# GpSimd's product with C and its sum into y as two instructions over two blocks each, in a state-space scan that VectorE, TensorE and GpSimd share

## The chip, the cores and the metric

The kernel runs on 1 core of one Trainium2 chip. The metric is the device time of one launch in microseconds (us). Engines are named as in the profile: PE is TensorE, ACT is ScalarE, DVE is VectorE, POOL is GpSimd, SP is SyncE, which only issues DMAs here. SBUF is the on-chip memory of 128 partitions, PSUM the accumulator memory of eight banks.

## The reference

Two layers on 4096 tokens (2 sequences of 2048) of width 256. The first layer is a selective scan and a mixture of four experts, the second is an attention with 16 heads and a feed-forward net. The part that the change touches is the scan:

```
A_bar = exp(delta[..., None] * A)                  # decay, 512 channels x 16 states
Bx = delta[..., None] * Bm[:, :, None, :] * xb[..., None]
def step(h, inp):
    a_t, bx_t, c_t = inp
    h = a_t * h + bx_t
    y_t = jnp.sum(h * c_t[:, None, :], axis=-1)    # the sum over the 16 states
    return (h, y_t)
...
y = y + xb * Dp
out = y * jax.nn.silu(z) @ W_out                   # gate, then project
```

The sum over the states of h times C is what GpSimd computes.

## The kernel before

The first phase works on eight chunks of 512 tokens. The 512 channels of a chunk are four blocks of 128 partitions, so h, y, the decays and the like are tiles of 128 x 4 x 512 in float32, the four blocks side by side in each partition. Each engine runs its own program, written out by hand: for iteration i it goes through the 16 states n = 0 to 15 of chunk i, and between the states it does its share of the side work for the chunk after (f = i + 1: convolution, projections, delta), the chunk before (m = i - 1: gate, output projection, router and experts) and the one before that (q = i - 2: queries, keys, values). All waits are on semaphores; nothing is scheduled at run time.

For each chunk c and state n:

- ACT writes the decays of four blocks (L948), two states ahead at most.
- PE broadcasts row n of B to 128 partitions in PSUM (L603).
- DVE multiplies it with delta times x for each block (`b_times`, L1264) and scans each block over its 512 tokens (`scan`, L1273) into `h[:, n % 2]`. There are two buffers of h. The first scan of state n waits until GpSimd has added state n - 2 to y. After the fourth block `keep_state` (L1278) keeps the last column.
- SP loads row n of C as a broadcast into `c_sb[:, n % 2]`, once the product of state n - 2 is made.
- GpSimd waits for all four scans, multiplies h with C in place (`times_c`, L1486), and adds the products to y (`add_y`, L1497). The last instruction of each tells of the whole, so nothing waits for one block.

Between the states DVE has side work that reads and writes SBUF: `gated` (L1288, y times the gate, 2048 elements), `crossed` (L1367), the keys' scaling in `keys` (L1376, two instructions), `weigh` (the router's weights: L1319, six comparisons at L1325, L1333, on 4 to 16 elements), `split_bias` (L1383 to L1389, four instructions of 512 elements on 16 partitions), `split_bc` (L1239 to L1246, five of 512) and `deltas` (L1254 and L1256, twice each, 1024 elements). The order around them is

```
if n == 7 and inside(m):
    weigh(m)
...
if n == 9 and inside(q):
    split_bias(q)
```

GpSimd has side work too: the splitting of q and k into bfloat16 parts (L1550 to L1559, 1024 elements) and short steps of the norms (L1566 to L1571).

When the eight chunks are done, a short stretch finishes the last experts, and from about 1850 us the attention and the feed-forward net run, in which GpSimd only copies values (L227) and adds a bias (L2019 and L2023, 1024 elements).

Of the kernel before, what the change touches and what calls it, by code (L numbers as in the profile page):

```python
# [11 lines left out]
ALU = mybir.AluOpType  # L12
# [3 lines left out]
P = 128  # L16
B, L, D = 2, 2048, 256
TOK = B * L
CH = 512
# [5 lines left out]
DB = DI // P  # L25
# [209 lines left out]
C_RING = 2  # L235
# [6 lines left out]
def mamba_moe_qkv(nc, a, scr, sh, chunks=NCH):  # L242


    with ExitStack() as ctx:  # L245
        def sb(name, shape, dt=F32):
            return ctx.enter_context(nc.sbuf_tensor(name, shape, dt))
# [42 lines left out]
        y = sh.heads_v[:].rearrange("p (b t) -> p b t", b=DB)  # L290
        decay = blocks_of[:, 0:2 * CH * DB].rearrange("p (a b t) -> p a b t", a=2, b=DB)
        h = sh.vals[:, 0:2 * CH * DB].rearrange("p (a b t) -> p a b t", a=2, b=DB)
        c_sb = sb("c_sb", [P, C_RING, CH])
# [1185 lines left out]
        def _(pool):  # L1479
            def times_c(c, n):  # L1480
                pool.wait_ge(c_loaded[n % C_RING], 16 * (c * (NS // C_RING) + n // C_RING + 1))
                pool.wait_ge(s["h_ready"], (c * NS + n + 1) * DB)
                if (c + 1) % CB:
                    pool.wait_ge(s["state_kept"], (c - c // CB) * NS + n + 1)
                for m in range(DB):
                    last = nc.gpsimd.tensor_tensor(h[:, n % 2, m, :], h[:, n % 2, m, :],  # L1486
                                                   c_sb[:, n % C_RING, :], ALU.mult)
                last.then_inc(s["hc_ready"], 1)

            def add_y(c, n):  # L1490
                pool.wait_ge(s["hc_ready"], c * NS + n + 1)
                if n == 0:
                    pool.wait_ge(s["y_begun"], (c + 1) * DB)
                else:
                    pool.wait_ge(s["y_added"], c * NS + n)
                for m in range(DB):
                    last = nc.gpsimd.tensor_tensor(y[:, m, :], y[:, m, :], h[:, n % 2, m, :], ALU.add)  # L1497
                last.then_inc(s["y_added"], 1)

            def first_values():  # L1500
# [72 lines left out]
            def iteration(i):  # L1573
                f, m, q = i + 1, i - 1, i - 2
                for n in range(NS):
                    if inside(i):
                        times_c(i, n)
                    if n == 0 and inside(q):
                        scale("ln2", q)
                    if n == 1 and inside(m):  # L1580
                        scale("ln1", m)
                    if n == 12 and inside(i + 2):
                        scale("ln0", i + 2)
                    if inside(i):
                        add_y(i, n)
                    if n == 1 and inside(f):
                        mix_edge(f)
                    if n == 6 and inside(f):
                        add_edge(f)
                    if n == 8 and isinstance(i, int) and i == chunks:  # L1590
                        first_values()
                    if 4 <= n < 8 and inside(q):
                        split(q, 0, q_f[:], n - 4)
                    if 9 <= n < 13 and inside(q):
                        split(q, 1, k_f[:], n - 9)
# [525 lines left out]
```

## Time and profile before

| | before |
|---|---|
| median of 3 runs | 3641.55 us (3640.53 to 3644.67) |
| the profiled execution, its own time | 3645.86 us |
| its span in the profile | 3644.1 us |
| PE busy in the span | 3312.8 us (91%) |
| DVE busy | 2839.1 us (78%) |
| ACT busy | 2176.2 us (60%) |
| POOL busy | 1527.7 us (42%), nearly all of it before 1640 us |
| mean granted clock of PE | 0.963 of full |
| POOL L1486, product with C | 512 instructions, 681.5 us |
| POOL L1497, sum into y | 512 instructions, 648.0 us |

The shares are averages over phases that have different limits. The phase that the change touches lasts from about 68 to 1620 us, and is read by itself below. An instruction's duration in the profile includes time in which it had begun and stood.

### The profile page before, as it was taken

Reading aid. Unit: us, or ns where it says so; the run is one execution under the profiler, and the core shown is the slowest. Engines: PE = TensorE matmul, PEld = TensorE weight load, DVE = VectorE, ACT = ScalarE, POOL = GpSimd, SP = SyncE. Lnnn points to the kernel's source line nnn. Section 1 sums busy time; section 2 is a strip of 40 time slices with the busy share of each in tenths; the row PEclk is TensorE's granted clock in tenths of the full one; section 3 lists DMA queues with packets and bytes.
Section 4 is the critical chain, followed back from the end, with each engine's and each line's share of the span. In section 5 each row is a group of like instructions: output and inputs, shape, how many; then the busy total and the mean of one; then the engine's idle time right before and its main releaser. Section 6 shows DMA issues by size and latency. Waiting matters only on the chain. (4 is left out here: it accounts for less than half of the span.)

```text
span 3644.1 us, 41261 instructions
## 1 busy us (share of the span) xinstructions
PE 3312.8 (91%) x14448; PEld 1552.3 (43%) x14448; DVE 2839.1 (78%) x3484; ACT 2176.2 (60%) x3604; POOL 1527.7 (42%) x1294
## 2 busy tenths in 40 slices
PE   4239999999999999989889999999999999998998
PEld 2025556555655555555522222322222222222666
DVE  5898899999989899974468888888888888882444
ACT  5355666656565756532157777777777777777221
POOL 2998899999999999971010000000000000000110
PEclk8679999999999999999999999999999999999999
DMA  3111223131222212232020000000000000000010
GB/s 109 32 38 52 73 70 102 63 112 64 94 84 82 87 62 93 73 121 85 26 97 19 19 19 19 19 17 17 15 17 19 19 19 19 19 10 7 23 35 29
DMA packets 108187, 180.19 MB, mean 49 GB/s; under 512 B 13989, under 2 KB 81689, under 8 KB 99417
## 3 DMA queue, kind: packets, MB, share of 16 engines
q1 hardware_dynamic: 107992, 177.72, 15.5%
q8 instruction: 108, 1.77, 0.2%
q14 instruction: 87, 0.70, 0.1%
HBM read 151.58 MB, written 26.08 MB: 49 GB/s over the span
## 5 line engine op out<-in xcount | busy, mean ns | idle before, releaser
L1927 DVE TENSOR_REDUCE tile_max<-ps 128x1 f32<-128x1024 f32 x976 | 1149.9, 1220 | 248.2 <-PE ps L1723 248.2
L1866 ACT ACTIVATE probs<-ps 128x512 f32<-128x512 f32 x2048 | 1106.4, 598 | 375.4 <-PE ps L1736 373.8
L1486 POOL TENSOR_TENSOR vals<-vals,c_sb 128x512 f32<-128x512 f32 x512 | 681.5, 1363 | 131.9 <-DVE state L1278 111.0
L1273 DVE TENSOR_TENSOR_SCAN vals<-stacks,state,ps 128x512 f32<-128x512 f32 x512 | 655.0, 1279 | 103.0 <-POOL heads_v L1497 38.1
L1736 PE MATMUL ps<-stacks 101*128 101x512 bf16 x2048 | 701.8, 382 | 24.7 <-PEq L245 12.2
L1497 POOL TENSOR_TENSOR heads_v<-heads_v,vals 128x512 f32<-128x512 f32 x512 | 648.0, 1298 | 8.7 <-issue 0.2
L1723 PE MATMUL ps<-stacks 99*128 99x512 bf16 x1952 | 583.8, 380 | 0.0
L227 POOL COPY heads_v<-vals 128x256 f32<-128x256 f32 x32 | 12.7, 402 | 1344.7 <-PE ps L1746 1322.2
L1746 PE MATMUL ps<-probs,heads_v 128*32 128x512 f32 x4096 | 545.3, 605 | 0.0
L731 PE MATMUL ps<-x1T,e_w 128*128 128x512 f32 x1024 | 464.1, 599 | 26.2 <-ACT hid L1041 26.2
L1736 PEld LDWEIGHTS ps<-stacks 101*128 101x128 bf16 x2048 | 195.7, 96 | 658.9 <-ACT probs L1866 423.2
L755 PE MATMUL ps<-e_w,hid 128*128 128x256 f32 x2048 | 455.0, 380 | 10.8 <-DVE x_tok L1355 8.8
L755 PEld LDWEIGHTS ps<-e_w,hid 128*128 128x128 f32 x2048 | 390.0, 191 | 84.7 <-issue 31.5
L1041 ACT ACTIVATE hid<-ps,cols 128x512 f32<-128x512 f32 x288 | 192.2, 687 | 390.1 <-PE ps L731 376.4
L731 PEld LDWEIGHTS ps<-x1T,e_w 128*128 128x128 f32 x1024 | 192.0, 191 | 261.0 <-issue 210.3
L1723 PEld LDWEIGHTS ps<-stacks 99*128 99x128 bf16 x1952 | 191.4, 98 | 172.5 <-issue 1.9
L948 ACT ACTIVATE stacks<-stacks,neg_a 128x512 f32<-128x512 f32 x256 | 167.0, 713 | 60.7 <-DVE vals L1273 60.2
L948 ACT ACTIVATE stacks<-vals,neg_a 128x512 f32<-128x512 f32 x256 | 166.3, 712 | 55.8 <-DVE vals L1273 50.3
L1264 DVE TENSOR_TENSOR ps<-soft,ps 128x512 f32<-128x512 f32 x256 | 177.2, 692 | 11.4 <-PE ps L603 3.2
L1264 DVE TENSOR_TENSOR ps<-stacks,ps 128x512 f32<-128x512 f32 x256 | 177.3, 693 | 7.0 <-issue 0.2
L2023 POOL TENSOR_TENSOR y<-x,b 128x1024 f32<-128x1024 f32 x8 | 19.3, 2417 | 377.6 <-DVE x L88 377.6
L603 PE MATMUL ps<-bc,sel 96*128 96x512 bf16 x128 | 52.1, 409 | 126.5 <-DVE ps L1264 112.1
(201 smaller groups left out, 3055.1 us busy)
## 6 DMA issues: line engine op xcount, KB each, us to landing
e_w<-in_e_w SPq DMA_DIRECT2D x64, 1024.0 KB, 7.1
c_sb<-scratch_c SPq DMA_DIRECT2D x128, 256.0 KB, 3.4
stacks<-scratch_q SPq DMA_DIRECT2D x192, 64.0 KB
stacks<-scratch_k SPq DMA_DIRECT2D x192, 64.0 KB
scratch_q<-parts SPq DMA_DIRECT2D x16, 384.0 KB, 4.2
scratch_k<-parts SPq DMA_DIRECT2D x16, 384.0 KB, 4.4
xr<-scratch_x SPq DMA_DIRECT2D x10, 512.0 KB, 4.4
xn_tok<-in_x SPq DMA_DIRECT2D x8, 512.0 KB, 4.9
```

The source lines that it names most:

```text
L731: last = mm(bank(key), e_w1[:, e % 2, k, i * P:(i + 1) * P], x1T[:, k, :], start=k == 0, stop=k == KD - 1)
L755: last = mm(ps[:, DOWN_BANK[at], i * D:(i + 1) * D], hid[:, k, (2 * pair + i) * P:(2 * pair + i + 1) * P], e_w2[:, e % 2, k, :], start=k = ...
L948: fn(decay[:, n % 2, m, :], deltas_at[c % 2][:, m, :], ACT.Exp, scale=neg_a[:, n * DB + m:n * DB + m + 1]).then_inc(s["decay_ready"], 1)
L1264: v.tensor_tensor(ps[:, 0, :], dus_at[c % 2][:, m, :], ps[:, 2 + n % 2, :], ALU.mult).then_inc(s["bx_ready"], 1)
L1273: v.tensor_tensor_scan(h[:, n % 2, m, :], decay[:, n % 2, m, :], ps[:, 0, :], state[:, n, m:m + 1], ALU.mult, ALU.add).then_inc(s["h_ready ...
L1486: last = nc.gpsimd.tensor_tensor(h[:, n % 2, m, :], h[:, n % 2, m, :], c_sb[:, n % C_RING, :], ALU.mult)
L1497: last = nc.gpsimd.tensor_tensor(y[:, m, :], y[:, m, :], h[:, n % 2, m, :], ALU.add)
L1723: last = mm(ps[:, at + i, :], qs[0:K_MAX, u % ROT, t * P:(t + 1) * P], ks[0:K_MAX, u % ROT, k * CH:(k + 1) * CH], start=True, stop=True)
L1736: mm(ps[:, S_BANK[i], :], ks[0:K_ALL, j, step * P:(step + 1) * P], qs[0:K_ALL, j, qc * CH:(qc + 1) * CH], start=True, stop=True).then_inc( ...
L1746: last = mm(ps[qc * VW:(qc + 1) * VW, AV_BANK, :], vh[:, u % ROT, step, :], probs[:, step % 2, qc, :], start=step == 0, stop=step == KT - 1)
L1866: fn(probs[:, step % 2, qc, :], ps[:, S_BANK[i], :], ACT.Exp)\
L1927: v.tensor_reduce(tile_max[:, t, half:half + 1], ps[:, at:at + PAIR, :].rearrange("p a n -> p (a n)"), AX.X, ALU.max).then_inc(s["max_read ...
```

## The change

The four instructions of 512 elements per partition in `times_c` become two of 1024, and so do the four in `add_y`. C is read with a repeat over the two blocks. Elements, order of the states, waits and semaphore counts stay as they are.

```diff
-                for m in range(DB):
-                    last = nc.gpsimd.tensor_tensor(h[:, n % 2, m, :], h[:, n % 2, m, :],
-                                                   c_sb[:, n % C_RING, :], ALU.mult)
+                for m in range(0, DB, 2):
+                    last = nc.gpsimd.tensor_tensor(h[:, n % 2, m:m + 2, :], h[:, n % 2, m:m + 2, :],
+                                                   c_sb[:, n % C_RING:n % C_RING + 1, :].to_broadcast([P, 2, CH]),
+                                                   ALU.mult)
                 last.then_inc(s["hc_ready"], 1)
...
-                for m in range(DB):
-                    last = nc.gpsimd.tensor_tensor(y[:, m, :], y[:, m, :], h[:, n % 2, m, :], ALU.add)
+                for m in range(0, DB, 2):
+                    last = nc.gpsimd.tensor_tensor(y[:, m:m + 2, :], y[:, m:m + 2, :], h[:, n % 2, m:m + 2, :],
+                                                   ALU.add)
                 last.then_inc(s["y_added"], 1)
```

## Rows read from the trace of the kernel before

**Rows 1.** The page: busy time of the engines, and the loads of C.

```profile
PE 3312.8 (91%) x14448; PEld 1552.3 (43%) x14448; DVE 2839.1 (78%) x3484; ACT 2176.2 (60%) x3604; POOL 1527.7 (42%) x1294
...
c_sb<-scratch_c SPq DMA_DIRECT2D x128, 256.0 KB, 3.4
```

**Rows 2.** Busy time in two stretches; the columns are PE, PEld, DVE, ACT, POOL.

```profile
430.00:1430.00 1000.00, 955.48 (x3200) 570.70 (x3199) 914.01 (x1143) 624.05 (x911) 931.99 (x776) 0.99 0.26 82
1430.00:1620.00 190.00, 173.89 (x595) 109.06 (x595) 158.47 (x186) 93.48 (x135) 179.04 (x146) 0.95 0.26 82
```

**Rows 3.** What DVE waited for, 430 to 1430 us: total, times, longest.

```profile
DVE vals L1273 <- POOL heads_v L1497: 12.2, 10, 2.2
DVE vals L1273 <- ACT stacks L948: 10.8, 6, 2.2
DVE x_tok L1355 <- PE ps L755: 7.8, 5, 2.4
DVE vals L1254 <- ACT soft L1012: 2.3, 2, 1.3
```

**Rows 4.** What PE waited for longest, 430 to 1430 us.

```profile
PE ps L731 <- ACT hid L1041: 21.1, 15, 1.7
```

**Rows 5.** POOL's instructions in order of time, states 1 and 2 of chunk 4.

```profile
851.87 4.96 POOL L1486 TENSOR_TENSOR vals<-vals,c_sb 128x512 f32<-128x512 f32 x4 [1.41 <-DVE state L1278]
...
869.66 4.97 POOL L1497 TENSOR_TENSOR heads_v<-heads_v,vals 128x512 f32<-128x512 f32 x4
```

**Rows 6.** DVE's in order of time: the first scan of state 4.

```profile
874.66 1.28 DVE L1273 TENSOR_TENSOR_SCAN vals<-stacks,state,ps 128x512 f32<-128x512 f32 x1 [2.09 <-POOL heads_v L1497]
```

**Rows 7.** POOL lines one by one: least, median and greatest duration in ns.

```profile
L1571 POOL TENSOR_TENSOR ln_t<-ln_half,ln_r x24: 200/203/204, 8.2 to 1805.8; 128x4 f32<-128x4 f32 x24
```
```profile
L1497 POOL TENSOR_TENSOR heads_v<-heads_v,vals x512: 1255/1270/2261, 73.6 to 1615.8; 128x512 f32<-128x512 f32 x171
```
```profile
L2023 POOL TENSOR_TENSOR y<-x,b x8: 2348/2353/2865, 3350.3 to 3596.1; 128x1024 f32<-128x1024 f32 x8
```
```profile
L1553 POOL TENSOR_TENSOR q_f<-q_f,parts x8: 2122/2136/2304, 506.9 to 1829.7; 128x1024 f32<-128x1024 f32 x8
```

**Rows 8.** DVE's L1385, its durations, and once beside a POOL instruction of 1024 elements.

```profile
L1385 DVE TENSOR_TENSOR soft<-soft x5: 680/1647/2489, 548.1 to 1841.2; 16x512 f32<-16x512 f32 x5
```
```profile
1841.20 2.49 DVE L1385 TENSOR_TENSOR soft<-soft 16x512 f32<-16x512 f32 x1
```
```profile
1840.94 2.21 POOL L1553 TENSOR_TENSOR k_f<-k_f,parts 128x1024 f32<-128x1024 f32 x1
```

**Rows 9.** DVE in order of time: the weights of the router, chunk 4.

```profile
921.37 0.91 DVE L1319 TENSOR_TENSOR prob<-lexp,lmax 128x16 f32<-128x16 f32 x1
922.32 3.76 DVE L1325 TENSOR_TENSOR beats<-prob 128x12 f32<-128x12 f32 x6
...
926.41 0.95 DVE L1333 SCALAR_TENSOR_TENSOR cw<-rank,prob 128x16 f32<-128x16 f32 x1
```

**Rows 10.** POOL in order of time, the same stretch and after.

```profile
920.99 4.99 POOL L1486 TENSOR_TENSOR vals<-vals,c_sb 128x512 f32<-128x512 f32 x4 [0.18 <-DVE state L1278]
926.05 4.96 POOL L1497 TENSOR_TENSOR heads_v<-heads_v,vals 128x512 f32<-128x512 f32 x4
...
946.66 6.24 POOL L1486 TENSOR_TENSOR vals<-vals,c_sb 128x512 f32<-128x512 f32 x4
```

**Rows 11.** Other side work of DVE line by line: least, median, greatest in ns.

```profile
L1288 DVE TENSOR_TENSOR gate<-heads_v,gate x8: 2293/2880/2889, 242.5 to 1617.1; 128x2048 f32<-128x2048 f32 x8
```
```profile
L1376 DVE TENSOR_SCALAR k_f<-k_f,temp x16: 475/958/2344, 511.3 to 1839.2; 128x512 f32<-128x512 f32 x16
```
```profile
L1241 DVE TENSOR_TENSOR q_f<-bc_f,bc x8: 689/1643/1645, 36.0 to 1376.9; 96x512 f32<-96x512 f32 x8
```
```profile
L1256 DVE TENSOR_TENSOR stacks<-stacks,vals x8: 1224/2172/2181, 52.5 to 1211.5; 128x1024 f32<-128x1024 f32 x8
```

**Rows 12.** What DVE waited for, 242 to 430, 68 to 242 and 1430 to 1620 us.

```profile
DVE x_tok L1355 <- PE ps L755: 4.3, 2, 3.4
DVE vals L1273 <- ACT stacks L948: 3.0, 2, 1.8
```
```profile
DVE vals L1273 <- POOL heads_v L1497: 12.4, 8, 2.8
```
```profile
DVE vals L1273 <- POOL heads_v L1497: 11.8, 7, 3.6
```

## The prediction, made before the changed kernel ran

> **What bounds the kernel now.** I read the page first: PE is busy for 91% of the span and POOL for 42% [rows 1], but POOL's work with C lies in the first phase, so I went on to busy times by stretch. Between 430 and 1430 us, five periods of 200 us in the middle of the scan, PE is busy for 955 us of 1000, POOL for 932 and DVE for 914 [rows 2]. Three engines near their limit: the waits must say which of them ends last. DVE's list shows 12.2 us on POOL's sum, 10.8 and 2.3 us on ACT and 7.8 us on PE [rows 3], with small rests some 37 us, 7.4 us a period: 2.4 on POOL and 4.9 on ACT and PE. Its other idle time, 86 - 37 = 49 us, is the gap of about 0.1 us between its instructions. PE's longest wait is for ACT's gelu [rows 4], which itself waits its turn behind decays.
>
> In order of time the period reads so. In states 1 to 3 POOL is behind: its products and sums run without a gap from 851.87 to 874.63, and the first scan of state 4 waits 2.09 us for the sum of state 2 [rows 5, 6]. In states 5 to 15 the path runs over PE and ACT, and DVE follows with 4.9 us of slack. So POOL sets the end in a short part of each period, and DVE is 5 us away from setting the rest.
>
> **What the change saves on POOL.** Instructions on float32 take 203 ns for 4 elements, 1270 for 512, 2353 for 1024 [rows 7]. The first two give (1270 - 203) / 508 = 2.10 ns an element, and 203 + 2.10 x 1020 = 2345 for 1024, which is the third. So the cost is per element, with a fixed part. Four in a row take 4.96 us [rows 5]: one starts every (4.96 - 1.27) / 3 = 1.23 us. Two make 2.46; one of 1024 takes a turn of 2.35 less the overlap of 0.04, 2.31. The saving is 0.15 us for each pair. The other bound is the 1024 elements of L1553, 2.13 us, whose second input is bfloat16 [rows 7]: 2.09 a turn, 0.37 us a pair. I take 0.15, since L2023 has float32 on all sides, as here.
>
> There are 512 pairs, 79 us of POOL's time, but only those in stretches where POOL is behind count. In a period these are the 16 instructions from 851.87 to 874.63 (two products, two sums of four) [rows 5]: 8 pairs, 1.2 us. In the first and the last chunk, where DVE waits for POOL 12.4 and 11.8 us [rows 12], I count half of the 128 instructions, 32 pairs or 4.9 us each; in chunk 1 some 11 pairs, 1.7 us. Together 4.9 + 1.7 + 5 x 1.2 + 4.9 = 17.5 us. With 0.37 a pair it would be 42 us.
>
> The loads of C cost nothing new: each is issued when a product ends, lands in 3.4 us [rows 1], and is wanted two products and two sums of waiting later, over 9 us with the longer instructions too. Nothing waits for single blocks, before or after.
>
> **What it costs on DVE.** DVE's side work takes longer beside POOL than alone. L1385 takes 680 ns alone, 1647 as a rule in the loop, and 2489 where a POOL instruction of 1024 elements had begun just before it [rows 8]. That POOL instruction ended at 1840.94 + 2.21 = 1843.15, and L1385 at 1843.69: it stood for 1.95 us and ran for 0.54. So it stands until POOL's instruction is over, whatever its length, and then runs. POOL's next one stands in turn: four products took 6.24 us in place of 4.96 at 946.66, where the four of `split_bias` ran [rows 10]. They alternate. Each DVE instruction behind such a turn loses what POOL's turn lasts, and this doubles: +1.08 us (2.35 less 1.27). One that comes at any moment loses half a turn on average, +0.54.
>
> By this, one period's side work:
> - `weigh`: product and sums run from 920.99 to 931.01, while L1319, the six at L1325 and L1333 take 5.99 us from 921.37 to 927.36 [rows 9, 10], on tiles of at most 16 elements. The six go in twos at each end of a POOL instruction. With instructions of 1024 the ends come at 923.3, 925.7, 928.1 and 930.5, so they finish near 931.1: +3.8.
> - `split_bias`, four in a row: the first stands behind a sum's end that comes 0.6 us sooner, three lose 1.08: +2.6.
> - `split_bc`, five, L1241 among them at 1643 for 689 alone [rows 11]: one stands behind a cast that stays short; three lose 1.08, and the first, which now slips in front of a POOL instruction, loses a little: +3.4.
> - `deltas`: L1256 stands at 2172 for 1224 alone [rows 11]; twice 1.08 and, for the two L1254, twice 0.54: +3.2.
> - `keys`, L1376, 2 x 1.08, as its one 2344 ns beside L1553 shows: +2.2. `gated`, at 2880 for 2293 [rows 11], begins just behind a product: +1.1. `crossed`: +0.5.
>
> The sum is 16.8 us. POOL will be at work for less of the time, so I take 0.9 of it, 15. The lower bound goes with the 2.13 us instruction, 0.86 in place of 1.08: 12.
>
> A rule bears on this, and speaks against the change. The Trainium skill (SBUF — State Buffer, section "Who interferes with whom") says that a VectorE instruction with two SBUF inputs contends with a GpSimd one that reads SBUF, and that whoever comes first keeps the pair of ports for its whole instruction. The trace agrees with 2489 against 1647 ns. By a rule in which the two only shared bandwidth, the length of an instruction would not matter, and the sum would be the saving alone, 17.5 us faster.
>
> **The sum.** A period of the five in the middle: +15 on DVE, less the 4.9 us that it waits for ACT and PE today, less 1.2 from POOL: +8.9. As a check: DVE's busy 183 + 15, its small gaps 9.8 and what is left of the wait on POOL, 1.2, make 209 against 200. Five of them: +45. Chunk 1 has no `keys` and no `split_bias`: (1.1 + 3.8 + 3.4 + 3.2) x 0.9 = 10.4, against 4.3 + 3.0 us [rows 12] and 6.3 of smaller waits on PE and ACT: covered, about 0 with POOL's 1.7. The first chunk has `split_bc` and `deltas` for the next: 5.9 - 4.9 = +1. The last has `keys`, `weigh`, `split_bias`: 7.7 - 4.9 = +2.8. Together +49 us. The attention is untouched. The profiled execution took 3645.86, 4.3 over the median of 3641.55; 3645.86 + 49 = 3695, and against the median 3690.5. I say 3690.
>
> **The rivals.** A change within 0.2% (7 us) can't be told from none.
> - *The saving decides, faster.* The place is the same side work: if DVE's slack swallows the longer stands, the time falls by 17.5 us, to 3624; with 0.37 a pair, to 3600. It decides once the added stands stay under 4.9 + 1.2 = 6.1 us a period, below 0.4 of what I count. For it: 4.9 us of slack, and POOL idle more often. Against it: a dozen of the instructions stand in chains, where POOL always has the next one ready. 0.12.
> - *The short 1024.* With 2.09 us a turn the period gives 12 - 4.9 - 2.9 = +4.2, five of them 21, and the ends -7, -4 and -6: +4, 3646. For it L1553, against it the line through three float32 rows. 0.08.
> - *Nothing is absorbed.* The stands fall where PE and ACT then wait for DVE's scans in turn: 16.8 - 1.2 = 15.6 a period, 78, and 10, 1 and 3 for the ends: 3734. PE's 45 us idle in 1000 [rows 2] would become over 100. 0.15.
> - My forecast, with a partial absorption of either sign: 0.65.
>
> **How the numbers follow.** The likeliest case has its own range from 3660, where half of the stands beyond the slack vanish, to 3725. The range of 8 in 10 goes from 3628 to 3735: it takes in the short 1024 and the upper case, and leaves out most of the faster one. Faster 0.12, same 0.08, slower 0.65 + 0.15 = 0.80.
>
> **What would show each step.** The product and the sum should have 256 instructions each, near 2350 ns; near 2130 would be the second rival. L1385 and L1241 should stand at 2.7 us, L1256 at 3.2, the six of L1325 near 7 us together for 3.76. POOL's busy time between 430 and 1430 should fall by 4 to 8 us in 100, DVE's should rise, and DVE's waits on PE and ACT nearly vanish, with PE idle longer. If L1385 stays at 1.65 us beside instructions of 1024, the whole cost side is wrong and the first rival holds. If the stands are as said and the period stays at 200 us, the slack was larger than DVE's waits show.

## The result, and the profile after

| | before | after |
|---|---|---|
| median | 3642.2 us (4 runs, 3640.53 to 3644.67) | 3699.39 us (4 runs, 3697.43 to 3702.77) |
| ratio after/before | | 1.0157, 95% interval 1.0141 to 1.0173 |
| span of the profiled execution | 3644.1 us | 3701.0 us |
| mean granted clock of PE | 0.963 | 0.957 |

The change makes the kernel 57 us slower; the prediction said 49 us slower, 3690 with a range from 3628 to 3735.

The page of the kernel after, busy time of the engines, beside [rows 1]:

```profile
PE 3336.5 (90%) x14448; PEld 1569.8 (42%) x14448; DVE 2932.4 (79%) x3484; ACT 2175.6 (59%) x3604; POOL 1450.5 (39%) x782
```

POOL works 77 us less, as its 512 instructions fewer should give (79 us were worked out), and DVE works 93 us more with exactly the same 3484 instructions. Nothing was added to DVE; its instructions stood longer, that is, they had begun and were held up.

The same stretch as in [rows 2]:

```profile
430.00:1430.00 1000.00, 925.60 (x3053) 552.68 (x3052) 943.21 (x1098) 592.66 (x870) 843.30 (x438) 0.97 0.24 78
```

DVE rises from 914 to 943 of 1000 us, PE falls from 955 to 926, POOL from 932 to 843; PE's granted clock is 0.97 for 0.99. What DVE waits for in this stretch, beside [rows 3]:

```profile
DVE vals L1273 <- POOL heads_v L1498: 4.7, 5, 1.0
...
DVE k_f L1372 <- PE ps L822: 1.5, 2, 1.3
DVE vals L1273 <- ACT stacks L948: 0.5, 1, 0.5
```

The 10.8 us on ACT's decays are 0.5, the 7.8 us on PE's experts are gone, and the 12.2 us on POOL are 4.7. PE waits for DVE instead, where [rows 4] had ACT on top (the wait of L675 for L1288 was 1.6 us before):

```profile
PE ps L755 <- DVE x_tok L1355: 20.3, 4, 5.2
PE ps L675 <- DVE gate L1288: 17.3, 5, 4.0
PE ps L731 <- ACT hid L1041: 15.5, 10, 1.7
```

By these waits DVE has become the engine that sets the pace; `pairs_but_7_9` below tests it. The lower clock of PE is not what sets it, since DVE waits for PE less than before. The lines one by one (least, median and greatest duration in ns), first POOL's sum and product, then the side work of [rows 8, 11]:

```profile
L1498 POOL TENSOR_TENSOR heads_v<-heads_v,vals x256: 2337/2356/3352, 73.7 to 1671.0; 128x1024 f32<-128x1024 f32 x128
...
L1486 POOL TENSOR_TENSOR vals<-vals,c_sb x256: 2336/2359/4418, 68.9 to 1666.3; 128x1024 f32<-128x1024 f32 x128
...
L1385 DVE TENSOR_TENSOR soft<-soft x5: 679/2728/2737, 553.7 to 1898.7; 16x512 f32<-16x512 f32 x5
...
L1241 DVE TENSOR_TENSOR q_f<-bc_f,bc x8: 687/1406/2729, 36.3 to 1426.9; 96x512 f32<-96x512 f32 x8
...
L1239 DVE CAST bc<-bc_f x8: 414/1610/1948, 35.9 to 1425.6; 96x512 bf16<-96x512 f32 x8
...
L1256 DVE TENSOR_TENSOR stacks<-stacks,vals x8: 1224/3257/3262, 52.9 to 1250.9; 128x1024 f32<-128x1024 f32 x8
...
L1288 DVE TENSOR_TENSOR gate<-heads_v,gate x8: 2291/4406/4421, 241.2 to 1673.4; 128x2048 f32<-128x2048 f32 x8
...
L1376 DVE TENSOR_SCALAR k_f<-k_f,temp x16: 477/1937/2578, 512.2 to 1896.7; 128x512 f32<-128x512 f32 x16
```

The least durations are those of before, within 10 ns; the medians moved. L1385 and L1256 grew by 1.08 us each, which is what POOL's instruction grew by, 2356 less 1270. L1241 did not go to 2.7 us as said: its median fell from 1643 to 1406 ns and only its longest is 2729, while the cast before it, L1239, went from 424 to 1610. The stands of `split_bc` changed places, and their sum comes out near the forecast (below). `weigh` in order of time, DVE and then POOL, beside [rows 9, 10]:

```profile
941.37 2.24 DVE L1319 TENSOR_TENSOR prob<-lexp,lmax 128x16 f32<-128x16 f32 x1
943.64 4.83 DVE L1325 TENSOR_TENSOR beats<-prob 128x12 f32<-128x12 f32 x6
...
948.79 1.92 DVE L1333 SCALAR_TENSOR_TENSOR cw<-rank,prob 128x16 f32<-128x16 f32 x1
```
```profile
941.22 4.67 POOL L1486 TENSOR_TENSOR vals<-vals,c_sb 128x1024 f32<-128x1024 f32 x2 [3.05 <-DVE state L1278]
945.96 4.71 POOL L1498 TENSOR_TENSOR heads_v<-heads_v,vals 128x1024 f32<-128x1024 f32 x2
```

It ends at 950.71, with POOL's last sum (950.67), 9.34 us after it began; before it took 5.99. The six comparisons take 4.83 us, not the 7 that were said: only two of them stand, for 2.28 and 2.32 us, and the other four pass in 0.15 us each, three of them one behind the other at the end of one POOL instruction. Before, three stood for 1.19 to 1.25 us. And POOL sat idle for 3.05 us ahead of the product, because the scans it waits for now come late.

### The profile page after: what moved, and what is told of

Its sections match the earlier page's. It is cut to its first block and busy times, and to the rows that moved or that the text cites. A ratio compares the mean times of both kernels' runs of the same rounds, so it can differ in the third digit from the quotient of the medians.

```text
span 3701.0 us, 40749 instructions
## 1 busy us (share of the span) xinstructions
PE 3336.5 (90%) x14448; PEld 1569.8 (42%) x14448; DVE 2932.4 (79%) x3484; ACT 2175.6 (59%) x3604; POOL 1450.5 (39%) x782
## 5 line engine op out<-in xcount | busy, mean ns | idle before, releaser
L1486 POOL TENSOR_TENSOR vals<-vals,c_sb 128x1024 f32<-128x1024 f32 x256 | 628.2, 2475 | 262.4 <-DVE state L1278 214.7
L1738 PE MATMUL ps<-stacks 101*128 101x512 bf16 x2048 | 701.6, 382 | 24.7 <-PEq L245 12.2
L1273 DVE TENSOR_TENSOR_SCAN vals<-stacks,state,ps 128x512 f32<-128x512 f32 x512 | 654.9, 1279 | 75.4 <-POOL heads_v L1498 20.4
L1498 POOL TENSOR_TENSOR heads_v<-heads_v,vals 128x1024 f32<-128x1024 f32 x256 | 622.2, 2451 | 8.5
L227 POOL COPY heads_v<-vals 128x256 f32<-128x256 f32 x32 | 12.6, 400 | 1344.7 <-PE ps L1748 1321.7
L755 PE MATMUL ps<-e_w,hid 128*128 128x256 f32 x2048 | 465.6, 386 | 36.9 <-DVE x_tok L1355 35.9
L731 PE MATMUL ps<-x1T,e_w 128*128 128x512 f32 x1024 | 466.7, 602 | 22.2 <-ACT hid L1041 21.7
L1738 PEld LDWEIGHTS ps<-stacks 101*128 101x128 bf16 x2048 | 195.6, 96 | 658.7 <-ACT probs L1868 422.9
L948 ACT ACTIVATE stacks<-stacks,neg_a 128x512 f32<-128x512 f32 x256 | 166.2, 713 | 53.8 <-DVE vals L1273 53.4
L1264 DVE TENSOR_TENSOR ps<-soft,ps 128x512 f32<-128x512 f32 x256 | 177.2, 692 | 14.1 <-PE ps L603 5.8
L1264 DVE TENSOR_TENSOR ps<-stacks,ps 128x512 f32<-128x512 f32 x256 | 177.3, 693 | 6.9 <-PE ps L603 0.4
```

What stands on the lines that cost most here:

```text
L731: last = mm(bank(key), e_w1[:, e % 2, k, i * P:(i + 1) * P], x1T[:, k, :], start=k == 0, stop=k == KD - 1)
L755: last = mm(ps[:, DOWN_BANK[at], i * D:(i + 1) * D], hid[:, k, (2 * pair + i) * P:(2 * pair + i + 1) * P], e_w2[:, e % 2, k, :], start=k = ...
L948: fn(decay[:, n % 2, m, :], deltas_at[c % 2][:, m, :], ACT.Exp, scale=neg_a[:, n * DB + m:n * DB + m + 1]).then_inc(s["decay_ready"], 1)
L1264: v.tensor_tensor(ps[:, 0, :], dus_at[c % 2][:, m, :], ps[:, 2 + n % 2, :], ALU.mult).then_inc(s["bx_ready"], 1)
L1273: v.tensor_tensor_scan(h[:, n % 2, m, :], decay[:, n % 2, m, :], ps[:, 0, :], state[:, n, m:m + 1], ALU.mult, ALU.add).then_inc(s["h_ready ...
L1486: last = nc.gpsimd.tensor_tensor(h[:, n % 2, m:m + 2, :], h[:, n % 2, m:m + 2, :], c_sb[:, n % C_RING:n % C_RING + 1, :].to_broadcast([P, ...
```

## Two numbers for each period

Two numbers make the experiments comparable. The *period* is the time from the first scan of one chunk to that of the next (L1273 in the timeline), the mean over chunks 2 to 6. The *stands* are, for the same stretch, the durations of DVE's side work at L1239 to L1256, L1288, L1309 to L1333, L1367, L1376 and L1383 to L1389, less the least duration that each line shows. The first scans of chunks 2 and 7 come at 429.8 and 1423.8 us before, 430.3 and 1476.1 after. Each ratio is to the runs of the kernel before in the same series, whose medians lie between 3642.2 and 3643.94 us.

| kernel | stands, us a period | period, us | median of runs, us | ratio to before |
|---|---|---|---|---|
| side_halves | 10.6 | 199.8 | 3655.34 | 1.0034 (1.0022 to 1.0047) |
| before | 17.8 | 198.8 | 3642.2 | |
| clean_pairs | 18.1 | 198.6 | 3637.86 | 0.9984 (0.9974 to 0.9994) |
| clean_more | 18.1 | 198.0 | 3635.34 | 0.9975 (0.9966 to 0.9984) |
| clean_fours | 18.4 | 198.0 | 3629.97 | 0.9958 (0.9944 to 0.9971) |
| sum_pairs | 23.1 | 199.3 | 3644.71 | 1.0004 (0.9994 to 1.0013) |
| pairs_but_7_9 | 27.7 | 203.5 | 3666.13 | 1.0063 (1.0046 to 1.0080) |
| product_pairs | 29.2 | 205.6 | 3681.56 | 1.0103 (1.0086 to 1.0120) |
| after | 33.6 | 209.2 | 3699.39 | 1.0157 (1.0141 to 1.0173) |
| side_pairs | 34.1 | 211.4 | 3718.47 | 1.0205 (1.0188 to 1.0222) |
| one_of_four | 53.4 | 228.2 | 3812.36 | 1.0466 (1.0449 to 1.0484) |

Up to some 23 us of stands the period stays between 198.0 and 199.8 us. The three `clean_` kernels are the same in these five chunks and differ by 0.6 us, so less than that can't be read from one trace. Beyond 23 us it grows nearly one for one: from sum_pairs to after 10.5 us of stands make 9.9 us of period, from after to one_of_four 19.8 make 19.1.

## The experiments

All use one form of the two functions, in which a width for each state says how many blocks go in one instruction (0.5 is half a block). As it adds lines to the kernel, GpSimd's line numbers differ from run to run; those of DVE stay:

```diff
-                for m in range(DB):
-                    last = nc.gpsimd.tensor_tensor(y[:, m, :], y[:, m, :], h[:, n % 2, m, :], ALU.add)
+                w = width("sum", c, n)
...
+                    for m in range(0, DB, w):
+                        last = nc.gpsimd.tensor_tensor(y[:, m:m + w, :], y[:, m:m + w, :], h[:, n % 2, m:m + w, :], ALU.add)
```

and the same for the product.

**side_pairs: long instructions only where the side work stands.**

```diff
+            SIDE_P, SIDE_S = (0, 5, 6, 7, 9, 12, 13, 14), (4, 7, 8, 11, 13)
+
+            def width(what, c, n):
+                return 2 if n in (SIDE_P if what == "product" else SIDE_S) else 1
```

> Two blocks in one instruction only where DVE's SBUF side work meets them: products of states 0, 5, 6, 7, 9, 12, 13, 14 and sums of states 4, 7, 8, 11, 13; all others stay at one block. Theory (DVE stands until POOL's instruction is over, and that instruction is 1.08 us longer): the whole loss of the full change stays, and the saving of POOL in states 1 to 3 is gone, so 57 + 6 = 63 us over before, 3698 to 3712 us; L1385 at 2.73 us, L1256 at 3.26. Rival (the loss comes from the long instructions as such, wherever they are): 13 of the 32 instructions of a chunk are changed, so 13/32 of 57, 23 us, 3665.

Measured: 3718.47 us, 75 over before. That is over the range of the theory by 6 us, and far from the rival's 3665: 13 of the 32 products and sums of a chunk carry more than the whole loss. L1385 stands as in the full change:

```profile
L1385 DVE TENSOR_TENSOR soft<-soft x5: 678/2728/2741, 558.8 to 1914.7; 16x512 f32<-16x512 f32 x5
```

**clean_pairs: the complement** (the lists are those of side_pairs).

```diff
+            def width(what, c, n):
+                return 1 if n in (SIDE_P if what == "product" else SIDE_S) else 2
```

> The complement: two blocks in one instruction for the products of states 1, 2, 3, 4, 8, 10, 11, 15 and the sums of the other eleven states, one block where DVE's side work stands. Theory: DVE's stands stay as before (L1385 1.65 us, L1256 2.17), POOL gives back 0.15 us for each of the 8 pairs of states 1 to 3 in six chunks, 7 us, and some 6 us in the first and the last chunk: 3629 us, 3624 to 3638. Rival: 19/32 of the 57 us, 34 us slower, 3676.

Measured: 3637.86 us, 5 us faster than before, at the slow edge of the range and far from the rival's 3676. The stands are those of before:

```profile
L1385 DVE TENSOR_TENSOR soft<-soft x5: 680/1643/2491, 547.4 to 1837.3; 16x512 f32<-16x512 f32 x5
```

So the place of the long instructions decides, not their number. But the gain is less than was said, and DVE's waits between 430 and 1430 us tell why:

```profile
DVE x_tok L1355 <- PE ps L755: 12.6, 5, 3.2
DVE vals L1273 <- ACT stacks L948: 10.9, 6, 2.2
DVE vals L1273 <- POOL heads_v L1512: 4.7, 5, 1.0
```

The wait on POOL fell by 7.5 us in five periods, 1.5 each where 1.2 were worked out. The wait on PE grew by 4.8, and DVE is busy for 917 of 1000 us where it was 914. POOL's saving in states 1 to 3 was handed on to a later wait; the period fell by 0.2 us. Most of the 5 us come from the ends: the first chunk takes 171.7 us for 173.8, the last 178.5 for 182.1.

**product_pairs and sum_pairs: one half of the change each.**

```diff
+            def width(what, c, n):
+                return 2 if what == "product" else 1     # sum_pairs: what == "sum"
```

> Two blocks in one instruction for all products, one for all sums. Theory: of the added stands of a period some 10.5 us stand behind products (gated 1.1, keys 2.2, half of weigh, split_bias, part of split_bc, three of deltas); less 4.9 us of slack and 0.6 saved it is +5 us a period, 25 us, and about 1 at the ends: 3668 us, 3655 to 3682. Rival (the read of C with a repeat is what costs, the stands do not): the product would stand for all of the 57 us, 3699.

> Two blocks in one instruction for all sums, one for all products. Theory: only 4.6 us of stands are added in a period, which DVE's 4.9 us of slack cover, and 0.6 us is saved: -0.9 us a period and some 4 at the ends, so 3633 us, 3628 to 3645. With product_pairs that makes 20 us where both together cost 57, since the slack is then spent once for both. Rival (no slack, every stand counts): 3642 + 20 = 3662.

Measured: 3681.56 us (+39) and 3644.71 us (+2, no difference that the runs tell). Each lies inside its range at the slow end; the theory's 20 us for both together are 40, against 57 for the full change. The stands are 11.4 and 5.4 us more than before, together 16.8 for the full change's 15.8, while the periods grow by 6.8 and 0.5 us, together 7.3 for 10.4. So the slack is there and is spent once, as was said, but both halves held more stands than I gave them. Both rivals fail: the product alone does not cost 57 us, so the repeated read of C is not what costs (L1486 with it and L1498 without take 2359 and 2356 ns), and sum_pairs does not cost the 20 us that it would without slack.

**one_of_four: all four blocks in one instruction.**

```diff
+            def width(what, c, n):
+                return 4
```

> All four blocks in one instruction of 2048 elements, product and sum. Theory: one takes 203 + 2.10 x 2044 = 4.50 us; each stand that is cut off by the end of POOL's work for a state (weigh, split_bias, split_bc) does not grow over that with two blocks, the others double again: some 25 us more DVE in a period than before, less 4.9 and 1.8: +19 us, 93 in five, 8 at the ends: 3743 us, 3710 to 3780. Rival (the fixed cost of an instruction decides): 26 us faster than before, 3616.

Measured: 3812.36 us, 170 over before, above the range. POOL's sum and L1385:

```profile
L1510 POOL TENSOR_TENSOR heads_v<-heads_v,vals x128: 4502/4526/5399, 74.1 to 1777.8; 128x2048 f32<-128x2048 f32 x128
```
```profile
L1385 DVE TENSOR_TENSOR soft<-soft x5: 680/4918/4924, 572.6 to 2006.1; 16x512 f32<-16x512 f32 x5
```

The size of one stand was right (4.50 us said, 4526 ns the median; beside the full change L1385 grew by 2.19 us for 2.17 of POOL). The count was wrong: the stands grew by 35.6 us over before, not 25, which is 19.8 over the full change where I gave 10. Of these, 6.1 fall in `weigh`, `split_bias` and `split_bc`, which I let grow no further (10.5 us for 8.1, 9.2 for 6.4, 7.5 for 6.6), and the other 13.7 nearly all in `deltas` (12.6 for 6.3), `keys` (7.3 for 3.4), `gated` and `crossed`. The rival, by which fewer instructions win, said 3616.

**side_halves: half blocks where the side work stands.**

```diff
+            def width(what, c, n):
+                return 0.5 if n in (SIDE_P if what == "product" else SIDE_S) else 1
```

> The other way: half a block (256 elements) in each instruction where DVE's side work stands (the products and sums of side_pairs), one block elsewhere. Theory: one takes 203 + 2.10 x 252 = 0.73 us, so each stand shortens by 0.5 us (L1385 to 1.1, L1256 to 1.6), but in a period the path runs there over PE and ACT, and only gated and crossed lie on it: -1 us a period, against 8 x 0.15 more POOL time where POOL is behind in the last chunk: 3630 to 3645, about 3638. Rival (DVE's side work sets the pace of the whole period, in both directions): -7 us a period, 3600.

Measured: 3655.34 us, 12 slower: a miss by 10 us on the theory's range, and against the rival altogether. The stands did shorten as said (L1385 to 1.10 us, L1256 to 1.63):

```profile
L1385 DVE TENSOR_TENSOR stacks<-stacks x3: 1095/1098/1102, 751.4 to 1546.6; 16x512 f32<-16x512 f32 x3
```

That freed 7.2 us of DVE in a period, and DVE's waits between 430 and 1430 us took them up:

```profile
DVE x_tok L1355 <- PE ps L755: 26.6, 10, 5.5
DVE vals L1273 <- ACT stacks L948: 11.8, 6, 2.2
DVE ps L1264 <- PE ps L603: 9.6, 7, 2.0
```

By these waits PE and ACT set the period of 199 us, and time that DVE saves below it is worth nothing. What I seem to have priced too low is POOL's side:

```profile
430.00:1430.00 1000.00, 957.76 (x3175) 570.15 (x3174) 875.75 (x1139) 618.07 (x902) 962.48 (x1032) 0.98 0.25 82
```

POOL is busy for 962 of 1000 us where it was 932. The first two chunks take 175.4 and 198.6 us for 173.8 and 195.6, and five in the middle 1.0 us more each. How much of this is POOL alone was not separated: PE's granted clock is also lower here, 0.98 for 0.99 in this stretch, and PE is busy for 958 us of 1000.

**pairs_but_7_9: the full change, spared where two side works stand.**

```diff
+            def width(what, c, n):
+                return 1 if (what, n) in (("product", 7), ("sum", 7), ("sum", 8), ("product", 9)) else 2
```

> The full change with one block in the product and sum of state 7, the sum of state 8 and the product of state 9, where weigh and split_bias stand. Theory: 3.8 + 2.6 us, 0.9 of it, leave DVE's 209 us period, which DVE sets: -5.8 us in each of six periods, 3699 - 35 = 3664, 3655 to 3675; their stands are back at 6.0 and 6.0 us in all. Rival (PE or ACT sets the 209 us period by now): 3695 or more.

Measured: 3666.13 us, 2 from the forecast, 33 us under the full change. The stands fell by 5.9 us a period and the period by 5.7, where the rival (PE or ACT sets it by now) said 3695 or more. DVE does set the pace of the changed kernel.

**clean_more and clean_fours: can a version beat both?**

```diff
+            def width(what, c, n):
+                if c == 0 and n < 11 or c == NCH - 1 and n > 9:
+                    return 2                             # clean_fours: 4
+                return 1 if n in (SIDE_P if what == "product" else SIDE_S) else 2
```

> clean_pairs, and in addition two blocks in one instruction for everything of states 0 to 10 of the first chunk and of states 10 to 15 of the last, where DVE has no SBUF side work. Theory: 26 more pairs at 0.15 us, 4 us, most of it where POOL is behind: 3 us under clean_pairs' 3638, 3632 to 3638. Rival (POOL's time there is covered, as it turned out to be in the middle chunks): as clean_pairs, 3638 to 3641.

> clean_more, with four blocks in one instruction in those states of the first and the last chunk. Theory: 22 states of product and sum less 5 with side work meet nobody's stand, each instruction saved gives 0.15 us, 34 of them 5 us, of which some 3 on the path: 3629 to 3636, the fastest of all. Rival (a longer instruction costs at its ends, since the scan of state n + 2 waits for the last of the sum and the next product starts later): 3640 or more.

Measured: 3635.34 us, ratio 0.9975 (0.9966 to 0.9984), and 3629.97 us, ratio 0.9958 (0.9944 to 0.9971), beside 3643.94 for before in the same series. Both lie in their ranges. For clean_more that shows little: its interval overlaps that of clean_pairs, and the rival began at 3638. clean_fours is clear of its rival's 3640, so longer instructions did not cost at their ends, and it is the fastest of all, 14 us under before. Its first chunk takes 167.8 us for 173.8, its last 176.3 for 182.1. What DVE waited for from 60 to 240 us in clean_fours, 12.4 us before [rows 12]:

```profile
DVE vals L1273 <- POOL heads_v L1513: 5.5, 7, 2.0
```

## Why the prediction was right, by its own steps

- **What bounds the kernel.** Right that DVE is near the pace and has some 5 us of slack in a period: the period stays flat from 17.8 to 23.1 us of stands and then rises. That POOL sets the end in states 1 to 3 was half right. DVE waits for it there, but what is saved there comes back as a wait on PE (clean_pairs).
- **The saving, term 1.2 us a period and 17.5 us in all: right in this kernel, not as a gain by itself.** The 0.15 us a pair is right: the new instructions take 2356 and 2359 ns against the 2345 worked out, and the second rival's 2130 did not come. DVE's wait on POOL fell from 12.4 to 7.8 us in the first chunk, from 1.7 to 0.4 in chunk 1, from 12.2 to 4.7 in 430 to 1430 us and from 11.8 to 7.7 in the last, 17.5 together. In the middle clean_pairs, with the stands of before, shows the same 4.7; at the ends part of the fall may be that DVE comes later, which was not separated. As a gain it is worth less as long as PE and ACT set the pace: clean_pairs has 19 of the 32 products and sums of a chunk and got 5 us, 0.2 a period. Where DVE sets the pace it counts: side_pairs, which lacks it, has a period 2.2 us over the full change's with only 0.5 us more stands. Its DVE waits 10.2 us for POOL in the stretch where the full change has 4.7, 1.1 a period, but also 4.1 us more for ACT, so not all of the 2.2 is POOL's. With pairs and fours at the ends too the gain came to 14 us.
- **The cost on DVE, 15 us a period.** Measured 33.6 less 17.8, 15.8; without the factor of 0.9 it was 16.8. By group, added against forecast before the factor 0.9: `weigh` 3.2 for 3.8, `split_bias` 2.7 for 2.6, `split_bc` 2.9 for 3.4, `deltas` 3.6 for 3.2, `keys` 2.1 for 2.2, `gated` 1.5 for 1.1, `crossed` 0.3 for 0.5, and the logits of the router, left out, 0.4 less. `weigh` and `split_bc` came out near for other instructions than I named (L1325, L1239 and L1241 above); that is in part luck. In the first two chunks the stands grew by less than the same prices gave, 1.9 us for 5.9 and 5.5 for 10.4.
- **The slack, 4.9 us.** The waits on ACT and PE went from 24.3 us in 430 to 1430 us to 2.6, and the bend lies between 5.4 and 9.9 us over before (sum_pairs, pairs_but_7_9).
- **The sum.** The five periods in the middle grew by 52 us for the 45 forecast, chunk 1 by 1.8 for 0, the last by 5.2 for 2.8; the first fell by 1.6, where +1 was said. Together they make 57 for 49. In the middle, 79 us of added stands less 21.7 us of waits on ACT and PE and 7.5 on POOL make 50 of the 52; of the 1.5 us a period that the forecast lacked, the factor of 0.9 is 0.8. POOL's busy time fell by 8.9 us in 100, more than the 4 to 8 that were said, since the longer period also spreads it.
- **The rivals.** That the saving decides is refuted: added stands of 15.8 us are past its point of 6.1. That nothing is absorbed is refuted by sum_pairs, whose 5.4 us of stands cost 0.5.

The Trainium skill (SBUF — State Buffer, section "Who interferes with whom") has the second of the two wait for the whole instruction of the first. The traces agree: a DVE instruction of 16 x 512 (L1385) took 1.10, 1.65, 2.73 and 4.92 us beside POOL instructions of 0.73, 1.27, 2.36 and 4.53 us.

## What to carry to other kernels

In this kernel the length of a GpSimd instruction was also the time for which VectorE's SBUF work stood. So before merging, look which instructions of VectorE run longer in company than their least duration, and at which steps of the loop. Merge where none of them runs and leave the rest: the same merge cost 75 us at the steps with such work and gained 5 at the others. Splitting there shortened the stands and still made the kernel 12 us slower, since VectorE had slack in any case and GpSimd had more to do; how much of the loss is GpSimd's was not separated. And work out how much slack the other engine has left: here a cost of up to 5 us a period was nearly free, what came above it counted nearly in full, and a saving below it mostly moved to the next wait.

## What the runs showed of the hardware that was not expected

VectorE instructions with one input in PSUM and one in SBUF did not stand in any of these kernels: the scan L1273 (decays in SBUF, B in PSUM) has a mean of 1279 ns before and after, and L1264 692 ns, with POOL at work beside them nearly all the time. Of 512 scans the longest takes 1282 ns in both. Casts and scalings with one float32 input in SBUF stood like those with two: L1243 and L1387 took 1.38 us before and 2.46 to 2.47 after, for 0.42 at the least. And POOL's cost per element was nearly the same from 4 to 2048 elements: 203, 726, 1270, 2353 and 4526 ns for 4, 256, 512, 1024 and 2048 elements lie within 1% of 203 ns and 2.10 ns for each element beyond the fourth.
